# Second bias of seven experts: TensorE's bias matmuls replaced by VectorE's additions to the sums in PSUM

## The reference

```python
scores, token_idx = jax.lax.top_k(flat_probs, k=capacity)      # 8 experts, 512 tokens each
tok = flat_x[token_idx]
h = jax.nn.gelu(jnp.einsum('ecd,edh->ech', tok, W1) + b1[:, None, :])
out_tok = jnp.einsum('ech,ehd->ecd', h, W2) + b2[:, None, :]
scaled = out_tok * scores[..., None]
routed = jnp.zeros_like(flat_x).at[token_idx.reshape(-1)].add(scaled.reshape(E * capacity, D))
```

## Time and profile before

| | |
|---|---|
| median of 3 runs | 893.98 us |
| profiled execution | 893.81 us, span 892.1 us |
| TensorE busy | 801.3 us (90%) |
| VectorE busy | 708.7 us (79%) |
| ScalarE busy | 767.8 us (86%) |
| GpSimd busy | 307.6 us (34%) |
| chain that ended last, by engine | PE 39%, ACT 38%, issue 11%, DVE 9% |

### The profile page before, as it was taken

How to read it: one execution, slowest core, us unless ns; L and a number is a source line. 1 busy time by engine, 2 the same in 40 slices (tenths; PEclk the granted TensorE clock), 3 DMA queues, 4 the chain that set the end, 5 groups by cost and what they waited for, 6 DMA issues and landing times.

```text
span 892.1 us, 14125 instructions
## 1 busy us (share of the span) xinstructions
PE 801.3 (90%) x5385; PEld 472.7 (53%) x5385; DVE 708.7 (79%) x1405; ACT 767.8 (86%) x601; POOL 307.6 (34%) x537
## 2 busy tenths in 40 slices
PE   7975679569998999999999999999988999999996
PEld 5321123124443444445454455545766899999986
DVE  5899889898989689988878995894887877676641
ACT  3989999999999999999999999997753677676672
POOL 3310540615543007674002740052203145555424
PEclk9899999999999999999999999999999999999998
DMA  8000000000001000200000010002202365544513
GB/s 267 19 1 0 1 1 1 1 24 15 10 9 40 1 1 25 71 2 1 24 1 1 25 48 1 24 1 89 77 24 78 98 181 142 136 106 132 137 20 41
DMA packets 32406, 41.82 MB, mean 47 GB/s; under 512 B 2365, under 2 KB 29011, under 8 KB 32339
## 3 DMA queue, kind: packets, MB, share of 16 engines
q1 hardware_dynamic: 26083, 32.49, 10.9%
q0 software_dynamic: 6144, 8.39, 5.7%
q10 hardware_dynamic: 112, 0.04, 0.0%
HBM read 28.33 MB, written 12.58 MB: 46 GB/s over the span
## 4 chain that ended last, share of the span: by engine, by line
PE 39%; ACT 38%; issue 11%; DVE 9%; POOL 1%; DMA 0%; POOLq 0%; ACTq 0%; DVEq 0%
ACT z L995 31%; PE bank L914 10%; PE bank L937 9%; PE bank L787 7%; DVE z L1372 4%; PE bank L829 3%; PE bank L844 3%; ACT z L991 2%; ACT u L1038 2%; PE bank L763 2%; PE bank L715 1%; PE bank L952 1%; PE bank L817 1%; ACT L1038 1%; PE bank L888 1%
## 5 line engine op out<-in xcount | busy, mean ns | idle before, releaser
L995 ACT ACTIVATE z<-z 128x4096 f32<-128x4096 f32 (+5 forms) x157 | 520.9, 3364 | 4.6 <-DVE z L1372 4.4
L1372 DVE TENSOR_SCALAR z<-feat,txt_bias 128x1024 f32<-128x1024 f32 (+1 forms) x722 | 421.9, 656 | 36.5 <-PE bank L787 35.6
L787 PE MATMUL bank<-z,window 128*32 128x512 f32 x2464 | 304.9, 604 | 64.0 <-ACT z L995 62.5
L787 PEld LDWEIGHTS bank<-z,window 128*32 128x32 f32 x2464 | 70.0, 110 | 249.7 <-issue 134.1
L844 PE MATMUL bank<-ws_sb,u 128*128 128x256 f32 x512 | 126.3, 387 | 5.6 <-ACT u L1038 5.6
L844 PEld LDWEIGHTS bank<-ws_sb,u 128*128 128x128 f32 x512 | 92.2, 189 | 41.1 <-issue 19.8
L829 PE MATMUL bank<-tr,ws_s 128*128 128x512 f32 x384 | 107.9, 417 | 0.0
L914 PE MATMUL bank<-xg_s,w_s 128*128 128x512 f32 x384 | 99.5, 397 | 0.2 <-DVE xg_s L1672 0.2
L937 PEld LDWEIGHTS bank<-w_s,hid_s 128*128 128x128 f32 x672 | 86.3, 188 | 4.0
L937 PE MATMUL bank<-w_s,hid_s 128*128 128x256 f32 x672 | 88.2, 280 | 0.0
L1074 ACT ACTIVATE hid<-bank,vec 128x512 f32<-128x512 f32 x64 | 44.2, 690 | 49.3 <-PE bank L914 49.2
(11 more groups left out here) (264 smaller groups left out, 750.4 us busy)
## 6 DMA issues: line engine op xcount, KB each, us to landing
w_raw<-in_L_ffn_W_dram SPq DMA_DIRECT2D x16, 1024.0 KB, 5.6
x_ring<-in_x_dram SPq DMA_DIRECT2D x8, 512.0 KB, 7.9
xn_dram<-xn SPq DMA_DIRECT2D x8, 512.0 KB, 2.9
out_dram<-x_ring SPq DMA_DIRECT2D x8, 512.0 KB, 3.2
u<-in_L_ffn_Ws_dram SPq DMA_DIRECT2D x1, 1024.0 KB, 11.0
ws_sb<-in_L_ffn_Ws_dram SPq DMA_DIRECT2D x1, 1024.0 KB, 13.7
xg<-xn_dram,idx POOLq DMA_INDIRECT x32, 4.1
out_dram<-y,idx POOLq DMA_INDIRECT x32, 3.9
```

The source lines that it names most:

```text
L787: ins = e.matmul(sums[v][32 * r:32 * r + 32, :], window[:, c, 31 - k:63 - k], z[:, n % ZB, at_piece:at_piece + TOK], start=(v, r) not in b ...
L995: e.activation(part, part, ACT.Tanh).then_inc(signal(*step), 1)
L1372: ins = e.tensor_scalar(z[:, n % ZB, i * width:(i + 1) * width], feat_of(units, c), bias_of(units, t, c), None, ALU.add)
```

## The change

`e_add`, a new step on VectorE, adds the second bias to the finished sums of experts 0 to 6. It reads a tile's sums from PSUM and the bias from `b2_rep`, a new SBUF tile that holds the seven bias rows in all 128 partitions, and writes `y`. `e_out` then multiplies `y` with the scores in place. The four bias matmuls of these experts go, and the first matmul of each bank starts it. `b2_rep` is filled by one transfer on SP behind the step `slots`. The wait for the scatter of two experts before moves from `e_out` to `e_add`, and TensorE waits for `e_add` instead of `e_out` before it uses a pair of banks again. Expert 7 keeps its bias matmuls.

```diff
-    order += [("slots",), high.pop(0)]
+    order += [("slots",), ("load_b2",), high.pop(0)]
...
                 for half in range(A // 2):
-                    order += [("e_sum", ex, half), ("e_out", ex, 2 * half), ("e_out", ex, 2 * half + 1)]
+                    order.append(("e_sum", ex, half))
+                    order += [step for a in (2 * half, 2 * half + 1) for step in (("e_add", ex, a), ("e_out", ex, a))]
...
+        b2_rep = sb("b2_rep", [P, E - 1, D])
...
+                elif kind == "load_b2":
+
+                    e.wait_ge(*done("slots"))
+                    e.dma_start(b2_rep[:].rearrange("p e d -> p (e d)"),
+                                b2[0:E - 1].rearrange("e d -> (e d)").partition_broadcast(P)).then_inc(loaded["b2_rep"], 16)
...
                         e.wait_ge(*done("split_lo", "w2", ex, PIECES[ex > 0] - 1))
-                        if ex == 0:
-                            e.wait_ge(*done("split_b2"))
                         if ex < 2:
                             sums_of = [take(bank) for bank in SUM[k]]
                         else:
-                            e.wait_ge(*done("e_out", ex - 2, A - 1))
+                            e.wait_ge(*done("e_add", ex - 2, A - 1))
                             sums_of = [banks[bank] for bank in SUM[k]]
-                        for a in range(A):
-                            e.matmul(sums_of[a // 2][:, a % 2 * D:(a % 2 + 1) * D], b2_row[:, ex:ex + 1].broadcast_to([B2_ROWS, P]), b2_s[:],
-                                     start=a % 2 == 0, stop=False, skip_group_check=True)
...
-                                           start=False, stop=(m == M - 1 and term == 2), skip_group_check=True)
+                                           start=(m == 0 and term == 0 and a % 2 == 0), stop=(m == M - 1 and term == 2),
+                                           skip_group_check=True)
...
-                    bank, left = (SUM[ex % 2][a // 2], a % 2 * D) if ex < E - 1 else (LAST_SUM[a], 0)
-                    e.wait_ge(*(done("e_sum", ex, a // 2) if ex < E - 1 else done("e_tile", a)))
                     e.wait_ge(*done("folded", ex))
-                    if ex > 1:
+                    if ex < E - 1:
+                        e.wait_ge(*done("e_add", ex, a))
+                        sums = y[:, ex % 2, a, :]
+                    else:
+                        e.wait_ge(*done("e_tile", a))
                         e.wait_ge(scattered, 16 * A * (ex - 1))
-                    e.activation(y[:, ex % 2, a, :], banks[bank][:, left:left + D], ACT.Identity,
-                                 scale=score[:, ex % NL, a:a + 1]).then_inc(signal(*step), 1)
+                        sums = banks[LAST_SUM[a]][:, 0:D]
+                    e.activation(y[:, ex % 2, a, :], sums, ACT.Identity, scale=score[:, ex % NL, a:a + 1]).then_inc(signal(*step), 1)
...
+                elif kind == "e_add":
+                    ex, a = args
+                    e.wait_ge(*done("e_sum", ex, a // 2))
+                    if ex == 0:
+                        e.wait_ge(loaded["b2_rep"], 16)
+                    elif ex > 1:
+                        e.wait_ge(scattered, 16 * A * (ex - 1))
+                    e.tensor_tensor(y[:, ex % 2, a, :], banks[SUM[ex % 2][a // 2]][:, a % 2 * D:(a % 2 + 1) * D], b2_rep[:, ex],
+                                    ALU.add).then_inc(signal(*step), 1)
```

More of the change, by code:

```diff
@@ L562, in xattn_moe_kernel @@
         }
-        BY_DMA = ("load_x", "load_w1", "load_w2", "store_xn2", "store_out", "gather", "scatter")
+        BY_DMA = ("load_x", "load_b2", "load_w1", "load_w2", "store_xn2", "store_out", "gather", "scatter")
         count, at = {}, {}
@@ L591, in xattn_moe_kernel @@
         loaded = {name: semaphore(f"ld_{name}") for name in
-                  ["w", "ctx", "ws", "b1", "bs1", "b", "Wcw", "Wcb", "w_col", "mask", "bcw", "bcb", "gate", "ws1", "ws2", "b2", *(f"x{v}" for v in range(UNITS)),
+                  ["w", "ctx", "ws", "b1", "bs1", "b", "Wcw", "Wcb", "w_col", "mask", "bcw", "bcb", "gate", "ws1", "ws2", "b2", "b2_rep", *(f"x{v}" for v in range(UNITS)),
                    *(f"{name}_{ex}" for name in ("w1", "w2") for ex in range(E))]}
```

## The result

The changed kernel takes 895.8 us (median of 20 runs, 895.51 to 897.8), against 893.98 before (20 runs). The ratio is 1.0017, with a 95% interval of 1.0011 to 1.0024: 0.2% slower, clear of the noise, and under the 0.3% that the prediction drew as its line. The profiled execution took 895.67 us with a span of 893.8, 1.7 longer than before. A few executions of either kernel (5 of 20 before, 4 of 20 after) take about 2 us more than the others, so medians are compared.

The account below looks back on a forecast made before the run. TensorE, busy 20.00 of 20.00 us while the experts run, was taken as the bound. Terms -0.46 - 0.46 + 2.15 + 1.05 = +2.3 gave 896.2 us as median, own range 895.0 to 897.4, whole range 892.0 to 898.3.

Parts of the forecast that it names:

- phase 0: First `e_down` of expert 0 to that of expert 1: no adds ahead, whole chain moves up, -0.46 us.
- phases 1 to 5: Between first `e_down`s of experts 1 to 6: late onehot delays the list's fourth quarter, 5 x 0.43 = +2.15 us.
- phase 6: From first `e_down` of expert 6 to the next: no list, VectorE has slack, -0.46 us.
- last expert: Expert 7: late gelus delay the last `e_lo`, TensorE waits in the first `e_tile`, +1.05 us.
- The matmuls' price: Four bias matmuls per expert removed from TensorE: 0.46 us each time, 3.2 us if nothing else is late.
- The adds: Four 128x256 adds per expert on VectorE: 0.425 us each, 0.345 start to start, PSUM costing nothing extra.
- Rival 3: Adds over 0.40 us apart pace ScalarE's `e_out`; at 0.50 apart, 898.1 us; chance 0.14.
- the bound for 0.60: Upper bound with adds 0.60 us start to start, first lasting 0.68: gelu of step 2 2.12 late.
- The wait: ScalarE's `e_out` waits for VectorE's adds behind `e_lo` of step 1, making the gelu of step 2 1.27 us late.
- The cover: VectorE's idle time ahead of the list's last onehot, 0.30 + 0.54 = 0.84 us, absorbs part of the late gelu.
- The load: Bias transfer of 0.92 MB on SP behind `slots`: lands near 672 us, wanted at 718, costs nothing.
- Rival 4: Bias load runs into the first gathers, first expert up to 1.5 us later: 897.7 us; chance 0.08.

Follow-up runs that it names:

- experiment 1: Kernel before without the 28 bias matmuls of experts 0 to 6 and no adds in their place: 890.7 us, ratio 0.9967.
- experiment 4: Changed kernel with the first two adds moved ahead of `e_lo` of step 1 in VectorE's order: 891.29 us, ratio 0.9967.
- experiment 6: Changed kernel with list, fold and gather of experts 2 to 7 put one step later in the order: 891.28 us, ratio 0.9978.
- experiment 3: Kernel before plus four VectorE adds of SBUF operands per expert, for which `e_out` does not wait: 894.02 us, ratio 1.0002.
- Experiment 5: Changed kernel with adds for experts 0 to 5 only, expert 6 keeping its bias matmuls and `e_out` from PSUM: 895.2 us, ratio 1.0015.

## Why the prediction was right, step by step

The forecast was 896.2, the measured median 895.8. (Two roundings in the forecast: 1.28 - 0.22 is 1.06, not 1.05, and the sum gives 896.3, not 896.2. Nothing hangs on them.) By steps, read from the same starts of TensorE in both traces:

| step | predicted | measured | from |
|---|---|---|---|
| before the experts | 0 | +0.09 | last `e_up` before the first `e_down`: 693.82 for 693.73 |
| phase 0 | -0.46 | -0.47 | list at 707.79 for 708.17 |
| phases 1 to 5 | +2.15 | +1.52 | `e_up` behind the list: 708.43 to 832.91 for 708.81 to 831.77 |
| phase 6 | -0.46 | -0.46 | last `e_sum`: 863.23 for 862.55 |
| last expert | +1.05 | +1.03 | first `e_tile`: 873.84 for 872.13 |
| sum | +2.3 | +1.7 | span 893.8 for 892.1 |

The 0.09 before the experts belongs to no step of the forecast and was not looked for.

**The matmuls' price** (0.46 for four) was right: -0.47 and -0.46 where nothing stands in the way, and 890.7 in experiment 1 where 893.98 - 3.2 = 890.8 was expected. In the order of the change the saving is used up by the wait; it arrives as soon as the hand-over is shortened (experiment 4) or the list asked for later (experiment 6).

**The adds** were sized right: 0.415 us each, four in 1.41, start to start 0.33; predicted 0.425 and 0.345. Reading PSUM costs VectorE no more than reading SBUF: 0.415 against 0.420 in experiment 3. The Trainium skill's 120 against 58 fixed cycles ("VectorE: DVE Perf Modes", section "The TRN2 errata — SBUF-src ops pay a fixed extra latency per instruction") do not show here. Rival 3, adds over 0.40 apart that pace ScalarE, fell: they are 0.33 apart. Its price was too low, though. It left out that at 0.50 start to start the first add lasts longer too, as the bound for 0.60 had it: the gelu would be 1.27 + 0.15 + 3 x 0.10 = 1.72 late, and the time about 899, not 898.1.

**The wait** was right in mechanism and nearly in size: gelu 2.74 - 1.40 = 1.34 late, predicted 1.27. Most of the 0.07 is the hand-over: the first add ends at 742.72 + 0.415 = 743.14 and `e_out` starts at 743.23, 0.09 later, where I had taken the 0.03 of a hand-over in the other direction. `e_out` from SBUF is as assumed: four in 1.71 with 0.50 for one, (1.71 - 0.50) / 3 = 0.40 start to start. Experiments 3 and 4 show that it is the wait, not VectorE's work.

**The cover** was the term that I sized wrong. From `e_lo` of step 2 to that of step 5 VectorE took 754.63 - 744.94 = 9.69 us before and 754.90 - 746.21 = 8.69 now: 1.00 was recovered, not 0.84. The bracket counts idle time from the end of the operation before. But an operation that waits for nobody starts about 0.08 before that end, so each of the two waits that vanished gave back its idle time and 0.08: 0.30 + 0.54 + 2 x 0.08 = 1.00.

Two small gains stand beside it. From the gelu of step 2 to its `e_lo` it is 746.21 - 744.85 = 1.36 instead of 1.39, and from `e_lo` of step 5 to the end of the last onehot 755.50 + 2.35 - 754.90 = 2.95 instead of 2.97. The late onehot is then 1.34 - 0.03 - 1.00 - 0.02 = 0.29, and the lists show just that: they are (832.91 - 733.34) / 4 = 24.89 us apart instead of 24.60. The first of the five phases has +0.35; 0.04 of the 0.06 more lies in the kernel before, whose first two lists are only 732.73 - 708.17 = 24.56 apart. So of the 2.15 forecast for five phases the cover takes 5 x 0.16 = 0.80, the small gains 0.25, and the longer wait gives 5 x 0.07 = 0.35 back. The errors partly cancelled, and the 1.52 lies nearer to the forecast than the cover alone would have put it.

**The last expert** had the right size at the wrong place. I put the wait into the first `e_tile`, for the last `e_lo`. The trace has it 5 us earlier: `e_up` of step 4 needs the PSUM bank that the gelu of step 2 empties. Before, that gelu ended at 865.53 + 0.69 = 866.22 and `e_up` of step 4 wanted the bank at about 863.97 + 12 x 0.23 = 866.7, a slack of 0.5. With the gelu 1.34 late, TensorE stands for 0.74 by the row and starts at 868.27 instead of 864.64 + 12 x 0.23 = 867.4, about 0.9 late. Most of the rest of the 1.03 comes at once, between the first and the second matmul of that step (868.27 and 868.61, where others are 0.23 apart). The wait that I had named, in the first `e_tile`, isn't there.

That the sums agreed (1.05 and 1.03) is luck. I let each later gelu be as late as the first, because ScalarE stood nowhere between them. But ScalarE now starts the first of them 1.23 to 1.24 apart instead of 1.36 (867.56, 868.79, 870.03): where it need not wait, its operations overlap as VectorE's do (`e_hi` ends at 868.25 + 0.63 = 868.88, the next gelu starts at 868.79). From the first of the six gelus to the last it took 872.33 - 865.53 = 6.80 us before and 874.04 - 867.56 = 6.48 now. With 0.32 made up on the way, the wait that I had worked out would have been about 0.7 instead of 1.05. Experiment 5 shows that the term is real: 0.46 back for four matmuls and 1.03 off, 895.2 expected and measured.

**The load** landed in 4.2 us from 666.7 and cost nothing: the first gather moved from 675.61 to 675.67. Rival 4 fell.

## What to carry to other kernels

Here, work moved from a full engine to one with over a quarter of idle time was paid at the hand-over, not in busy time. Look at the queue in which the new step stands, at who waits for it in order, and at the first place behind where the full engine needs the result: beside the 890.7 us without any adds, the same adds cost 5 us or 0.6, by where they stood in VectorE's order. An idle time in brackets was a little less than what could be recovered (0.84 read, 1.00 recovered), since an operation that needn't wait overlaps the one before. And where two engines pass work through two buffers, check the wait for the free buffer as well as the one for the data.

## What the runs showed of the hardware

A 128x256 add took VectorE 0.415 us with one operand in PSUM and 0.420 with both in SBUF. ScalarE's scaling of 128x256 took 0.498 us from SBUF and 0.476 from PSUM in the same kernel, less of a difference than 0.63 against 0.595 had made me expect. From the end of ScalarE's `e_hi` to the start of VectorE's `e_lo` it took 0.03 us, from the end of VectorE's add to ScalarE's `e_out` 0.09. A transfer that copies 7 KB into each of 128 partitions (896 KB) landed in 4.2 us, sooner than the 1 MB weight loads (5.8 us in the same execution). The granted clock of TensorE stayed at 1.00 (the 2.4 GHz level) through the holes of 0.67 us.
